# Adding the layer 1 mask on VectorE in every second score slot, in a four-layer cross-attention kernel

## What is computed

```python
q = (hidden_state @ Wq + bq).reshape(b, l, KVH, GROUPS, HD)      # 32 query heads of 16, in 8 groups of 4
k = (encoder_hidden_state @ Wk + bk).reshape(b, s, KVH, HD)      # 8 key heads
v = (encoder_hidden_state @ Wv + bv).reshape(b, s, KVH, HD)
scores = jnp.einsum('bkgld,bksd->bkgls', q, k) * scale
scores = scores + encoder_attention_mask[:, :, None, :, :]       # a full 512 x 512 fp32 mask per batch element
attn = jax.nn.softmax(scores, axis=-1)
out = jnp.einsum('bkgls,bksd->bkgld', attn, v)
out = out.reshape(b, l, H) @ Wo + bo
x = out + hidden_state                                           # then a layer norm
```

## Time and profile before

| | |
|---|---|
| median of 3 runs | 4301.14 us (4297.38 to 4302.05) |
| the profiled execution | 4311.11 us, span 4309.5 us |
| TensorE busy | 87% |
| VectorE busy | 35% |
| ScalarE busy | 27% |
| mean granted clock of TensorE | 0.943 of full speed |

### The profile page before, as it was taken

How to read it: one execution, slowest core, us unless ns; L and a number is a source line. 1 busy time by engine, 2 the same in 40 slices (tenths; PEclk the granted TensorE clock), 3 DMA queues, 4 the chain that set the end, 5 groups by cost and what they waited for, 6 DMA issues and landing times. The chain is left out here.

```text
span 4309.5 us, 39566 instructions
## 1 busy us (share of the span) xinstructions
PE 3736.4 (87%) x14128; PEld 1798.2 (42%) x14128; DVE 1525.2 (35%) x2792; ACT 1183.0 (27%) x1404; POOL 293.4 (7%) x228
## 2 busy tenths in 40 slices
PE   5998988889799898878979989887897989988799
PEld 2444533334344553333434455333343445533334
DVE  2415443530340544343034054434303305443430
ACT  1312323241131232324113133222412313322340
POOL 3000011000100001100010000110001000011000
PEclk9999999999899999989989999998998999999899
DMA  6322153311622215331162221533116221153401
GB/s 125 66 88 40 21 103 48 59 32 50 126 68 82 36 23 101 47 64 28 51 126 65 84 34 26 99 55 59 25 54 128 66 82 31 25 99 55 68 16 59
DMA packets 151761, 271.10 MB, mean 63 GB/s; under 512 B 15520, under 2 KB 22372, under 8 KB 151544
## 3 DMA queue, kind: packets, MB, share of 16 engines
q1 hardware_dynamic: 151556, 268.35, 30.8%
HBM read 152.95 MB, written 4.19 MB: 36 GB/s over the span
## 5 line engine op out<-in xcount | busy, mean ns | idle before, releaser
L908 ACT ACTIVATE pt<-score_banks 128x1024 f32<-128x1024 f32 x768 | 761.0, 1022 | 950.3 <-PE score_banks L769 482.4
L639 PE MATMUL bank<-xT,w 128*128 128x512 f32 x1664 | 755.4, 601 | 38.3 <-ACT xT L881 23.4
L1038 DVE TENSOR_REDUCE mcol<-bank 128x1 f32<-128x512 f32 x528 | 359.3, 689 | 469.7 <-PE bank L737 466.2
L639 PEld LDWEIGHTS bank<-xT,w 128*128 128x128 f32 x1664 | 315.9, 192 | 396.5 <-issue 370.4
L765 PE MATMUL score_banks<-qs,ks 99*128 99x512 f32 (+1 forms) x1280 | 450.7, 429 | 23.6 <-DMA qs<-nm_lo 12.6
L737 PE MATMUL bank<-ks,qs 97*128 97x512 f32 (+1 forms) x784 | 344.8, 453 | 137.7 <-DMA ks<-k_full 49.5
L1021 DVE TENSOR_REDUCE mcol<-score_banks 128x2 f32<-128x1024 f32 x248 | 301.7, 1223 | 426.2 <-PE score_banks L728 411.6
L838 PE MATMUL score_banks<-w,wide 128*128 128x512 f32 x1024 | 443.4, 592 | 0.0
L1035 DVE CUSTOM_DVE_ANT_0 bank<-bank,wide 128x512 f32<-128x512 f32 x416 | 284.7, 708 | 260.5 <-PE bank L737 259.9
L737 PEld LDWEIGHTS bank<-ks,qs 97*128 97x128 f32 (+1 forms) x784 | 155.0, 198 | 396.2 <-issue 349.1
L728 PE MATMUL score_banks<-ks,qs 97*128 97x512 f32 x496 | 275.4, 639 | 46.5 <-issue 23.8
(11 more groups left out here) (110 smaller groups left out, 3003.3 us busy)
## 6 DMA issues: line engine op xcount, KB each, us to landing
ks<-k_high SPq DMA_DIRECT2D x136, 256.0 KB, 5.7
w<-in_up SPq DMA_DIRECT2D x32, 1024.0 KB, 5.0
w<-in_down SPq DMA_DIRECT2D x32, 1024.0 KB, 5.3
qs<-q_high SPq DMA_DIRECT2D x112, 256.0 KB, 6.7
ks<-k_full SPq DMA_DIRECT2D x72, 256.0 KB, 7.8
w<-in_v SPq DMA_DIRECT2D x16, 1024.0 KB, 5.4
w<-in_q SPq DMA_DIRECT2D x16, 1024.0 KB, 8.1
qs<-q_full SPq DMA_DIRECT2D x64, 256.0 KB, 6.0
```

The costliest lines, as they stand in the source:

```text
L639: last = nc.tensor.matmul(o[:, :], wt[:, c, cols[0]:cols[1]], src[:, c, :], start=(c == 0), stop=(c == NC - 1))
L908: nc.scalar.activation(pt[:, i % PTB], score_banks[:, 2 * (i % 2):2 * (i % 2) + 2, :], ACT.Exp, scale=L.scale).then_inc(exp_done, 1)
L1038: ins = nc.vector.tensor_reduce(col, bank[:, :], AX.X, ALU.max)
```

## The change

In the odd slot of every group of layer 1, TensorE no longer issues the identity products; its score product stops the accumulation. VectorE adds the transposed fp32 mask to both heads of the slot in place, in PSUM, with one instruction of 128 x 1024, and ScalarE's exponential of that slot waits for it (`masked`) in place of `score_full`. The even slots are as before. For the addition there is an exact copy of the transposed mask, `maskT32`, in `wide[:, 1]`: ScalarE makes it with a second copy in each `maskT` step, and VectorE frees the ring bank only when both copies are made. The wait on `down_done` keeps the copy from the last MLP product that reads `wide[:, 1]`.

```diff
+MASKED_AT = {s: i + 1 for i, s in enumerate([s for s in SCORE_STEPS if s[1] == 1 and s[3] % 2])}
...
+        maskT32 = wide[:, 1]
...
@@ TensorE, score step
-                                                        q_of(g)[0:L.row + 3, j, :], start=True, stop=n != 1)
-                                if n == 1:
+                                                        q_of(g)[0:L.row + 3, j, :], start=True, stop=n != 1 or s % 2 == 1)
+                                if n == 1 and s % 2 == 0:
                                     nc.tensor.matmul(o, ident_r[:, :], maskT[:, 0, kt, :], start=False, stop=False)
                                     last = nc.tensor.matmul(o, ident_r[:, :], maskT[:, 1, kt, :], start=False, stop=True)
@@ ScalarE, maskT step
                             act.wait_ge(pv_done, last_pv(unit_at(0, 3)))
+                            act.wait_ge(down_done, N_DOWN[("down", 0, NFB - 1)])
                             nc.scalar.activation(maskT[:, 0, step[1], :], ring_bank(step)[:, :], ACT.Copy).then_inc(maskT_high, 1)
+                            nc.scalar.activation(maskT32[:, step[1], :], ring_bank(step)[:, :], ACT.Copy).then_inc(maskT_full, 1)
@@ ScalarE, score step
-                            act.wait_ge(score_full, i + 1)
+                            if n == 1 and step[3] % 2:
+                                act.wait_ge(masked, MASKED_AT[step])
+                            else:
+                                act.wait_ge(score_full, i + 1)
@@ VectorE, maskT step
                             dve.wait_ge(maskT_high, step[1] + 1)
+                            dve.wait_ge(maskT_full, step[1] + 1)
@@ VectorE, score step (there was none)
+                        elif kind == "score" and step in MASKED_AT:
+                            i = SINDEX[step]
+                            dve.wait_ge(score_full, i + 1)
+                            pair = score_banks[:, 2 * (i % 2):2 * (i % 2) + 2, :]
+                            nc.vector.tensor_tensor(pair, pair, maskT32[:, step[3] // 2:step[3] // 2 + 1, :].broadcast_to([P, 2, S]),
+                                                    ALU.add).then_inc(masked, 1)
```

More of the change, by code:

```diff
@@ L307, in build @@
         maskT_high = sem("maskT_high")
+        maskT_full = sem("maskT_full")
+        masked = sem("masked")
         exp_done, pv_done = sem("exp_done"), sem("pv_done")
```

## The result

| | before | changed |
|---|---|---|
| median of the runs | 4301.6 us (4 runs) | 4389.2 us (4 runs, 4375.3 to 4405.6) |
| ratio | | 1.0204, 95% interval 1.0166 to 1.0242 |
| the profiled execution, span | 4309.5 us | 4404.0 us |
| mean granted clock of TensorE | 0.943 | 0.906 |

The changed kernel is 2.0% slower, 88 us on the medians. The forecast was 18 us slower, 4319.5 us in a range up to 4352; the time is 37 us above the range.

A forecast was written before the change was run, and what follows sets the result against it. TensorE bounds the kernel before; after the change, waits for ring banks behind VectorE's addition take back its savings. Terms without the clock +8.8 us, clock +9.6, sum +18.4 on 4301.1: 4319.5 us, range 4284 to 4352.

The forecast's parts named there:

- Products removed: Odd slots of layer 1: 128 identity products fewer a pass, 120 us in all if nothing else bound.
- the addition: VectorE's mask addition on 128 x 1024: expected to take 1.23 us, occupying VectorE for 1.15.
- the two kinds of group: Layer 1 groups: with four maxima 4.88 us against 4.94; with five, 6.21 between additions against 5.2 plus a 0.7 stall.
- the walk: Step list of the 25 intervals between first and 26th pv in layer 1, carried through with the expected durations.
- the bank chain: Ring bank behind the addition: next maximum starts 1.15 us after the addition's start, its bank is refillable 0.90 later.
- The fill at full clock: Layer 1, first to 26th pv: gains and losses of its groups sum to +3.7 us a pass.
- First group: First group of layer 1, ahead of any VectorE backlog: gains 0.8 us a pass.
- last pairs: Last five even-odd slot pairs of layer 1, without maxima, and the last pv: 2.2 us a pass shorter.
- The opening: Start of a pass: the second mask copy delays the first q product by 1.5 us, bounds 0.5 and 2.2.
- The clock: TensorE's clock in layer 1: one more fall to half rate per pass, 2.4 us each, +9.6 us in all.
- Rival 2: Clock falls behind most fifth maxima too, five more falls a pass in place of one: 4358 us, chance 0.17.
- rival 1: Same waits behind the addition but no further fall of the clock: 4309.9 us, chance 0.24.

The follow-up runs named there:

- e8: Changed kernel with 5 unneeded TensorE products before a group's fifth max step and 4 or 7 before a maxT step, none before the first: 4280.9 us, ratio 0.9952.
- e9: Changed kernel without VectorE's addition, so the odd slots leave the mask out; the opening's second copies stay: 4277.9 us, ratio 0.9946.
- e2: Kernel before with only the second mask copy of the opening added; all score slots still use identity products: 4307.8 us, ratio 1.0020.
- e7: Changed kernel with 2 unneeded TensorE products before each group's first max step, none before the fifth max or maxT steps: 4334.1 us, ratio 1.0073.

## Why the prediction was wrong

*Products removed, the addition, the two kinds of group*: right. 512 products are gone, the addition takes 1.249 us (1.23), the first plain group 4.84 (4.88), plain groups at full clock in e8 4.47 to 4.83 (the walk's eleven had 4.68 on average), and the bank chain shows 1.14 and 0.89 us (1.15 and 0.90). That the 120 us do not come through was right too, and e9 adds that most of them would not have come without the addition either.

*The fill at full clock, +3.7 us a pass*: right. The fill of the kernel before took 154.6 us, of which the walk left out 7.0 as the clock's (183.6 - 176.6); with 3.7 that is 151.3. e8 has 151.3 with 7 to 10 us at the lower clock, and the changed kernel carried back to none has about 150.

*First group -0.8, last pairs -2.2*: measured -0.7 and, in the one pass with full clock there, 21.2 to 19.0. In the other three the clock fell in it, and they took 22.8.

*The opening, +1.5 a pass*: 2.1 by e2, and 3.0 in the changed kernel itself, where the early maxima also run slower for a while. The copies take 0.60 us, not 0.54.

*The clock, "I take one more fall per pass", 4 x 2.4 us*: this is the step that failed, in the number of the falls and in their length. In place of one more fall a pass there were five (28 in the four fills, against 7). One was taken as 6.8 us; together they added 67 us a pass at half clock (267.7 / 4), ten times as much. The price of such a us was near, 0.29 us measured and 0.35 assumed. At 0.29 the fills lose 77 us to the clock, and by difference 69 us (83.9 less four times 3.7), in place of 9.6.

The walk had the waits in the right places, with 1.6 us before a fifth entry and 2.25 before a closing `maxT`; measured were 1.2 to 1.5 and 1.8 to 1.9. What was wrong is what they do. I let only one of them cost the clock, because 1.31 us alone had not; but it fell beside 26 of the 36 of 1.2 us and more that found it full. And I took a fall to end after 6.8 us, as in the earlier trace rows, while here one lasted 41 us with TensorE busy nearly all the time, and e7 shows that the small waits have a part in the length.

Rival 2, at a chance of 0.17, was the right one in its mechanism: it had five more falls a pass, behind the fifth maxima, where 18 of the 28 are, and the sign that the prediction gave for it, a clock of 0.5 there, is seen (1.51 us at 375.88, then 0.50). Its 4358 is 31 us too low, mainly since it too priced a fall at 6.8 us. The Trainium skill's rule by which the sum would have been rival 1's (TensorE: Matmul & The Clock Gate, "HAM oscillation"), that longer gaps than these cost the clock, does not account for these falls: the longest wait of the fill in the first pass was 1.82 us.

## What to carry to other kernels

Taking work off a busy TensorE is no gain where its next step waits for a buffer that the relieved work's new owner frees: follow one buffer around the loop, and put the added instruction behind those that free buffers only if the order can bear it. Then ask what the new waits do to the clock, how many falls they make and how long each lasts: here most began beside waits of 1.2 to 1.9 us, and filling the small waits made them shorter. A few products that nobody needs, in the waits and no longer than they are, tell in one run whether the clock is the loss.

## What was not expected of the hardware

The clock fell in a group where TensorE waited 0.31, 0.24 and 1.07 us, and behind a single wait of 1.20 us, and had stayed where it waited 1.31 alone. The same wait of 1.06 us cost it in one pass and not in another. Once down, it stayed at half for 41 us while TensorE was shown busy in 39.2 of them, so that being the bound again did not by itself bring it back. And one execution had 66 to 114 us of its fill at half clock from pass to pass. That may be why the runs of the changed kernel are spread over 30 us, where the four of the kernel before beside them were within 11 (later sets of 11 and 12 runs of it within 21), but no run shows it.
